# Sparse feed-forward: weights kept in natural column order, TensorE loads every fourth column

## What is computed

```python
def _sparsify_2to4(h):
    B, S, I = h.shape
    g = h.reshape(B, S, I // 4, 4)
    a = jnp.abs(g)
    _, idx = jax.lax.top_k(a, 2)
    pos = jnp.arange(4)
    mask = (pos == idx[..., 0:1]) | (pos == idx[..., 1:2])
    return (g * mask.astype(g.dtype)).reshape(B, S, I)

h = jax.nn.silu(jnp.einsum('bsh,hi->bsi', x, w_gate)) * jnp.einsum('bsh,hi->bsi', x, w_up)
h_sparse = _sparsify_2to4(h)
return jnp.einsum('bsi,ih->bsh', h_sparse, w_down)
```

## Time and profile before

| | us |
|---|---|
| median of 3 runs | 1826.97 |
| lowest and highest | 1826.77, 1828.30 |
| the profiled execution | 1828.67 |
| its span, first to last instruction | 1826.9 |
| TensorE / VectorE / ScalarE / GpSimd busy | 1698.9 / 1385.8 / 1133.9 / 632.1 |
| granted TensorE clock, mean | 0.977 |

### The profile page before, as it was taken

The page is one execution under the profiler, slowest core; times in us unless marked ns, Lnnn a source line. Parts: engine busy times, 40 slices in busy tenths (PEclk is TensorE's granted clock), DMA queues, the critical chain, the costliest instruction groups (busy, mean ns, idle before and its releaser), DMA issues. The chain is left out here.

```text
span 1826.9 us, 29555 instructions
## 1 busy us (share of the span) xinstructions
PE 1698.9 (93%) x9152; PEld 1309.2 (72%) x9152; DVE 1385.8 (76%) x2105; ACT 1133.9 (62%) x2120; POOL 632.1 (35%) x507
## 2 busy tenths in 40 slices
PE   5999999999999999999999898879899899897998
PEld 4777787778787878778877787656457655456887
DVE  6777777777777777777775665888888788886996
ACT  3555655565556555555555553799996899883442
POOL 2332333232323232323221111049784089690000
PEclk9999999999999999999999998989999999998999
DMA  2000000000000000000000100023220122140000
GB/s 94 18 30 18 23 17 29 17 23 17 27 15 24 16 25 14 23 25 15 15 6 1 48 0 1 3 81 104 81 92 12 38 92 103 70 138 1 1 24 24
DMA packets 25088, 64.12 MB, mean 35 GB/s; under 512 B 2816, under 2 KB 8960, under 8 KB 24768
## 3 DMA queue, kind: packets, MB, share of 16 engines
q1 hardware_dynamic: 25024, 63.31, 10.5%
HBM read 60.94 MB, written 2.36 MB: 35 GB/s over the span
## 5 line engine op out<-in xcount | busy, mean ns | idle before, releaser
L2024 POOL TENSOR_SCALAR prob<-prob,rinv 128x640 f32<-128x640 f32 (+7 forms) x256 | 213.5, 835 | 674.3 <-DVE rinv L1423 673.2
L2100 POOL TENSOR_TENSOR m_h<-m_h,m_C 128x1024 f32<-128x1024 f32 x128 | 305.8, 2393 | 193.7 <-DVE m_h L1902 193.4
L1902 DVE TENSOR_TENSOR_SCAN m_h<-m_y,ps 128x1024 f32<-128x1024 f32 x128 | 291.5, 2284 | 52.7 <-PE ps L841 48.2
L968 ACT ACTIVATE prob<-prob,nmax 128x640 f32<-128x640 f32 (+7 forms) x256 | 198.3, 774 | 192.6 <-DVE nmax L1417 192.5
L526 PE MATMUL ps<-pt,v_sb 128*128 128x512 f32 (+3 forms) x768 | 310.3, 486 | 1.9 <-ACT pt L975 1.7
L975 ACT ACTIVATE pt<-ps 128x512 f32<-128x512 f32 (+3 forms) x384 | 186.0, 484 | 151.3 <-PE ps L516 150.1
L848 PE MATMUL ps<-m_h,ident 128*128 128x512 f32 x512 | 250.2, 612 | 11.3 <-POOL m_h L2100 11.3
L1417 DVE CUSTOM_DVE_ANT_0 prob<-prob,bias 128x640 f32<-128x640 f32 (+7 forms) x256 | 204.6, 799 | 44.9 <-issue 27.6
L516 PEld LDWEIGHTS ps<-ident,prob 128*128 128x128 f32 x1152 | 145.6, 140 | 116.6 <-issue 87.5
L1412 DVE TENSOR_SCALAR prob<-ps 128x640 f32<-128x640 f32 (+7 forms) x256 | 192.4, 752 | 42.3 <-PE ps L497 40.4
L1289 ACT ACTIVATE m_u<-m_uT,m_bT 128x256 f32<-128x256 f32 x512 | 210.6, 495 | 8.6 <-PE ps L841 8.6
(11 more groups left out here) (227 smaller groups left out, 3471.9 us busy)
## 6 DMA issues: line engine op xcount, KB each, us to landing
m_C<-bc_dram SPq DMA_DIRECT2D x64, 512.0 KB, 3.6
wqk_raw<-wqk_in SPq DMA_DIRECT2D x16, 512.0 KB, 3.2
wv_raw<-wv_in SPq DMA_DIRECT2D x16, 256.0 KB, 2.6
wo_raw<-wo_in SPq DMA_DIRECT2D x16, 256.0 KB, 2.9
x<-x_in SPq DMA_DIRECT2D x2, 1024.0 KB, 6.8
q_raw<-wgu_in SPq DMA_DIRECT2D x8, 256.0 KB, 2.8
raw<-wgu_in SPq DMA_DIRECT2D x1, 2048.0 KB, 8.4
out<-x SPq DMA_DIRECT2D x8, 256.0 KB, 2.2
```

The lines of the kernel that those rows point to most:

```text
L968: nc.scalar.activation(prob[:, at:at + n], prob[:, at:at + n], ACT.Exp, bias=nmax[:, k:k + 1], scale=-1.0, accum_out=rsum[:, k:k + 1]).the ...
L1902: nc.vector.tensor_tensor_scan(m_h[:, 2 * (v % 2) + e, :], m_da[:, 2 * (v % 2) + e, :], drive(e), 0.0, ALU.mult, ALU.add).then_inc(scan_do ...
L2024: nc.gpsimd.tensor_scalar(prob[:, at:at + n], prob[:, at:at + n], rinv[:, k:k + 1], 1.0, ALU.mult, ALU.mult).then_inc(norm_done, 1)
L2100: nc.gpsimd.tensor_tensor(state, state, m_C[:, v, :], ALU.mult).then_inc(hc_done, 1)
```

## The change

Two places change. `weight_chunks()` no longer reorders: ScalarE and VectorE read raw, and write gu_hi and gu_lo, contiguously, so that gate and up columns keep their natural order. In `gate_up` the stationary operand is then a slice with a step of 4: columns at, at + 4, ..., at + 508, where at = 4 * (u % 2) * 128 + e. The words of one slice are 16 bytes apart.

```diff
-                at = (2 * e + u % 2) * P
+                at = 4 * (u % 2) * P + e
...
-                                              (gu_hi, gu_lo)[w][:, k, half * F + at:half * F + at + P],
+                                              (gu_hi, gu_lo)[w][:, k, half * F + at:half * F + at + 4 * P - 3:4],
...
-                    whole, halves = raw[:, at + c:at + c + S], [t[:, c:c + S] for t in (flat_hi, flat_lo)]
-                    if not at:
-                        whole = whole.rearrange("p (g e) -> p e g", e=4)
-                        halves = [t.rearrange("p (e g) -> p e g", e=4) for t in halves]
-                    parts.append((whole, *halves))
+                    parts.append((raw[:, at + c:at + c + S], flat_hi[:, c:c + S], flat_lo[:, c:c + S]))
```

## The result

The change made the kernel slower: 1837.73 us median of 6 runs (1834.22 to 1838.96) against 1827.63 of 6 runs of the kernel before on the same chip (1824.56 to 1829.66). The ratio is 1.0052, 95% interval 1.0040 to 1.0064, which is +9.5 us (+7.3 to +11.7). The forecast was 1836, slower by +8.6.

The account below looks back on a forecast made before the run. The weight-copy chain bounds the preparation, TensorE most of the last stage. Copies -2.6, loads +10.8 and +1.5, tail -1.1 sum to +8.6 us: 1837.3 for the profiled execution, 1835.6 at the median, range 1823 to 1845.

Parts of the forecast that it names:

- Head copies: Feed-forward weight preparation: one gu_hi and two gu_lo copies on the chain become contiguous and cheaper, -2.6 us.
- TensorE's last add: Before the second m_xc: this add ends at 1647.08, m_xc would start at 1647.7, so the whole -2.6 us stands.
- Output matmuls: The 96 matmuls after the copies: shorter idle time may keep the clock at 2.4 GHz; 0 in sum, -1.4 in range.
- Loads at 256 columns: Last unit's 96 gate/up matmuls: strided loads stretch the spacing from 120 to 230-236 ns, +10.8 us.
- The extra 15 ns behind each load: Gate/up matmuls: 13 to 16 ns between matmuls may also stand behind a load; +1.4 and +4.8 us, range only.
- Loads at 512 columns: Gate/up matmuls before the last unit: spacing 229 to 230-236 ns over 321 matmuls, +1.5 us.
- Tail: End of the last unit: VectorE's slack behind ScalarE's g_sg is used up when TensorE is late, -1.1 us.
- Rival 1: Gate/up loads fetched early enough that the step costs nothing visible; 1824.4 us; chance 0.20 together with the case between.
- rival 2: Loads hidden and the output matmuls stay at 2.4 GHz: -4.0 us, 1823.0; chance 0.08.
- The load of 57 ns plus the step: Case between rivals 1 and 2: gate/up loads of 160 to 181 ns, 1828 us; chance 0.20 together with rival 1.
- Rival 3: Gate/up loads fetch each column twice, 460 ns a load: +104, about 1931 us; chance 0.12 with any load well over 250 ns.
- Rival 4: The change doesn't do what it says, because the compiler adds copies for the strided operand; given no chance.

Follow-up runs that it names:

- e1: The changed kernel with the stationary operand of gate and up contiguous again, cheap copies kept; 1824.68 us, ratio 0.9982 to the kernel before.
- v2: The kernel before with down weights split first and the last two low parts of gate and up on GpSimd; 1827.60 us, ratio 1.0002.
- e3: The changed kernel with the stationary operand read at a step of 2 words, not 4; 1825.05 us, ratio 0.9987 to the kernel before.
- e5: The changed kernel with contiguous stationary operands in the last unit only, step of 4 elsewhere; 1828.28 us, ratio 1.0008 to the kernel before.
- e6: The changed kernel with the stationary operand read at a step of 3 words, not 4; 1830.74 us, ratio 1.0020 to the kernel before.
- v1: The kernel before with the down weights split first and the strided gate and up copies after them; 1827.26 us, ratio 1.0000.
- v3: The kernel before with down weights split first, m_yh before ScalarE's last two copies, VectorE's last two low parts in first-norm gaps; 1826.20 us, ratio 0.9991.
- v4: The kernel before with its step of 4 shared out: copies read with a step of 2 words, loads with a step of 2; 1825.36 us, ratio 0.9988.
- e4: The changed kernel with the stationary operand read at a step of 8 words, not 4; 1840.21 us, ratio 1.0072 to the kernel before.
- e2: The kernel before with only the stationary operand read at a step of 4 words, copies left strided; 1841.55 us, ratio 1.0081.

## Why the prediction was right, point by point

The direction and the mechanism held: loads longer than the matmuls of 256 columns in front of them, against cheaper copies. The time held too, 1837.73 against 1836, but partly by luck: against the trace the terms were off by +1.9 and +0.5 one way and by -1.5, -0.6 and -0.4 the other, which cancels to -0.1.

**Head copies, -2.6 predicted, -2.14 measured.** The copies became what the earlier trace rows said. What was overlooked is what is late next: not TensorE's last add, which the earlier trace rows had named, but GpSimd's last product on m_h. GpSimd and VectorE in time, first the kernel after, then e1:

```profile
1643.28 2.35 POOL L2096 TENSOR_TENSOR m_h<-m_h,m_C 128x1024 f32<-128x1024 f32 x1 [0.25 <-DVE m_h L1898]
...
1645.08 1.63 DVE L1938 TENSOR_TENSOR gu_lo<-raw,gu_hi 128x1024 fp32r<-128x1024 f32 x1 [1.89 <-ACT gu_hi L1094]
```

```profile
1643.62 2.36 POOL L2096 TENSOR_TENSOR m_h<-m_h,m_C 128x1024 f32<-128x1024 f32 x1 [0.25 <-DVE m_h L1898]
...
1645.17 1.89 DVE L1938 TENSOR_TENSOR gu_lo<-raw,gu_hi 128x1024 fp32r<-128x1024 f32 x1 [1.63 <-ACT gu_hi L1094]
```

GpSimd ends at 1645.63 and 1645.98, VectorE's first low part at 1646.71 and 1647.06: 1.08 us later in both, though it was started 0.55 and 0.81 us before GpSimd's end. In this overlap VectorE makes next to no progress. The eight other traces with this overlap have 1.08 to 1.09 us as well, and so has v2's m_yl: its 5.27 us end at 1659.49, GpSimd's 7.10 at 1658.41. In the kernel before the slow copy kept VectorE away from GpSimd's product here, but its trace had the effect four times earlier, twice in each batch's scan. One of the four, VectorE and GpSimd in time, and the line of VectorE's scans:

```profile
1574.60 4.51 DVE L1935 TENSOR_TENSOR m_yl<-m_xc,m_yh 128x1024 fp32r<-128x1024 f32 x2
1574.76 3.27 POOL L2100 TENSOR_TENSOR m_h<-m_h,m_C 128x1024 f32<-128x1024 f32 x1 [0.75 <-DVE m_h L1902]
...
L1902 DVE TENSOR_TENSOR_SCAN m_h<-m_y,ps x128: 2253/2287/2289, 1207.3 to 1640.3; 128x1024 f32<-128x1024 f32 x128
```

VectorE's first m_yl had started before GpSimd's product and took its usual 1.2 us, and it is GpSimd that lost, 3.27 us and not 2.37; the second m_yl took 3.39 us and ended 1.08 us after GpSimd. VectorE's 128 scans, which read one operand from PSUM (ps), took 2.25 to 2.29 us with or without a GpSimd product beside them (112 lay for over 80% of their time beside one, 11 beside none). So it is the instructions with both inputs in SBUF that give way. The Trainium skill, "SBUF — State Buffer", section "SBUF: two separate sides", on the port pair that VectorE and GpSimd share, calls it an exclusive lock, under which the loser blocks; the rows agree.

**Output matmuls, 0 in the sum, -1.4 in the range, -1.50 measured.** The idle time before them fell from 4.48 to 2.62 us (1.9 was forecast) and in the profiled execution the 96 matmuls all ran at 2.4 GHz (granted clock 1.00 from 1650.29 to 1661.90). TensorE in time in the kernel after, then e3, where the chain gives the 96 as well:

```profile
1650.29 0.38 PE L882 MATMUL ps<-wout_hi,m_yh 128*128 128x256 f32 x1 [2.62 <-DVE m_xc L1921]
```

```profile
1648.41 0.39 PE L882 MATMUL ps<-wout_hi,m_yh 128*128 128x256 f32 x1 [2.62 <-DVE m_xc L1921]
...
1648.41 13.26 PE ps L882 x96
```

With the same 2.62 us of idle time, e3's took 13.26 us. Over the profiled executions, from the first to the last start, these 96 took 11.5 us in the kernel after, e1, e5, e6, v1, v3 and v4, 12.7 to 13.0 in e3, e4, v2 and before, and 14.2 in e2 (4.89 us idle). So the idle time alone doesn't settle it. What does is open, and whether it belongs to a kernel or to an execution too, since each kernel has one trace. The -1.50 is what this execution had; no run shows that the change brings it each time.

**Loads at 256 columns, +10.8 predicted, +10.41 measured.** The rate of the copies, 1.79 to 1.84 ns a column, carried over to TensorE's loads, 1.82. 96 loads at 233 and not 120 ns are +10.8, as forecast; the 0.4 less is time in which TensorE waited for VectorE in the kernel before, around 1791.5 in its last unit, and which the longer loads cover. The extra 15 ns behind each load, kept in the range, was not there: 128 columns at the copies' rate make 229 to 236 ns by themselves.

**Loads at 512 columns, +1.5 predicted, +3.44 measured: the step that failed.** The sum took every load of a block alike, beside a matmul of 512 columns, 1 to 7 ns too long. Eleven of twelve are so, at about 6 ns. But the first of a block that stands behind a down matmul of 256 columns is exposed like those of the last unit, by 345 - 233 = 112 ns. Per block that is 0.11 + 11 x 0.006 = 0.18, the 2.93 less 2.75 of the rows. 17 blocks stand so, and three more (two behind a transpose, one behind the last gate_up of the unit before) are longer by 0.17 to 0.19: 20 blocks make +3.6. The eight blocks before these give a little back, from the first L714 on 27.8 us and not 28.1, since fewer of their matmuls ran at the lower clock. TensorE in time in the kernel after, and the table of stretches with its header:

```profile
1672.77 1.05 PE L714 MATMUL ps<-g_xl,gu_hi 128*128 128x512 f32 x2
1673.62 1.05 PE L714 MATMUL ps<-g_xh,gu_hi 128*128 128x512 f32 x2
...
1676.01 0.63 PE L714 MATMUL ps<-g_xh,gu_hi 128*128 128x512 f32 x2
```

```profile
core 0: us, PE busy (x) PEld busy (x) DVE busy (x) ACT busy (x) POOL busy (x), PEclk, DMA share, GB/s
1670.90:1676.01 5.11, 5.11 (x12) 4.11 (x13) 0.00 (x0) 0.33 (x1) 0.00 (x0) 0.52 0.01 3
```

The pairs stand 0.85 us apart at the lower clock, the same as before, and at 1676.01, 5.11 us and 12 matmuls after the stage's start, the short ones are back; before it took 14 matmuls and 6.11 us.

**Tail, -1.1 predicted, -1.68 measured**: the slack as forecast, and 0.6 of clock in the last down matmuls.

**The rivals.** Rival 1 (load hidden, 2.88 and 2.75) fell with the first block; so did rival 2. The load of 57 ns plus the step, between them, would have given 160 to 181 ns; it is 233 for a step of 4, while a step of 3 lands there, at +3.7 us. Rival 3 (460 ns; its sum, 74 + 33 - 3.7, is +103 and not +104) is excluded by 5.60 / 24 = 233: no second fetch of a column shows. Rival 4 is excluded by the page: every engine has the same count of instructions as in the earlier trace rows.

## What to carry to other kernels

A strided stationary operand costs nothing as long as its load fits beside the matmul in front, so count the 16-byte pieces that it touches (here 1.82 ns each) against the shortest matmul that stands in front of any such load, the first of each block too, not against the usual one. Where a layout must be turned, split the step between the copy and the load: a step of two fp32 words was all but free on ScalarE, VectorE and TensorE, a step of four took 1.7 to 2 times as long on each (TensorE's as spaced at 256 columns). And when an instruction of VectorE with both inputs in SBUF is made shorter or moved, look at what GpSimd does at that time: the overlap is paid in full by whichever comes second.

## What the runs showed of the hardware that was not expected

- VectorE's subtraction of 1024 columns, started while GpSimd's product ran, ended 1.08 to 1.09 us after that product's end, with 0.29 to 0.89 us of overlap alike, and two of 1024 columns took 5.27 us beside GpSimd where they take 2.36 alone. VectorE's scans, with one operand in PSUM, took 2.25 to 2.29 us either way.
- At 256 columns the price of a strided load shows from a step of three words on: spacing 120 ns at steps 1 and 2, 174 to 179 at 3, 233 at 4, 240 at 8.
- Where TensorE is at the lower clock the step costs nothing: the matmuls of 512 columns at the start of the stage are spaced 427 ns before and after (0.85 us a pair).
- The same 2.62 us of idle time before the output matmuls was followed by 96 matmuls in 11.5 us in some traces and in 12.7 to 13.0 us in others.
